# Linear attention numerators taken for two batches in one product with 128 weight columns

## Chip, cores and metric

One core of a Trainium2 chip runs the whole program. The metric is device time of that core in microseconds (us), the median over executions. Traces are of one profiled execution.

## What is computed

The input x is 8 batches of 512 rows of 128. Four layers follow one another, each added to x: a delta-rule attention, a mixture of 8 experts (top 2), a linear attention, and the same experts again. The change is in the third of them. Its reference, with 16 heads of 8 (`q`, `k` after elu + 1), over chunks of the rows:

```python
def step(carry, inp):
    S, z = carry
    q, k, v = inp
    A = jnp.einsum('bhid,bhjd->bhij', q, k) * mask
    num = jnp.einsum('bhij,bhjd->bhid', A, v) + jnp.einsum('bhid,bhde->bhie', q, S)
    den = jnp.sum(A, axis=-1) + jnp.einsum('bhid,bhd->bhi', q, z) + EPS
    out = num / den[..., None]
    S = S + jnp.einsum('bhjd,bhje->bhde', k, v)
    z = z + jnp.sum(k, axis=2)
    return ((S, z), out)
```

## The kernel before

The kernel works in 8 chunks (`NCH`) of 64 rows (`CH`) of all 8 batches, so a chunk is 512 tokens, held as 4 groups (`J`) of 128 partitions: two batches of 64 rows each. Its first half (up to about 566 us) runs the delta-rule attention with the first experts. Its second half, `step2(i)` for i = 0 to 8, runs the linear attention of chunk i (i = 0 to 7) interleaved by hand with the second experts of the chunk before. Every engine has its own instruction list, written in a fixed order, and the lists meet only in semaphores.

In TensorE's list of `step2`, `moe_up` (L1004 to L1006, three products with 512 moving columns for each half of the hidden layer) and `moe_down` (L1024, 8 products with 128 moving columns) of the 8 experts alternate with the parts of the linear attention. For each group j of two batches:

- `lin_scores` (L1138) makes the scores A of both batches, in four quarter-size tiles of the array, into two PSUM banks. Partition 64·par + s holds key row s of a head of parity par.
- VectorE's `lin_att` (L1598) multiplies them by the causal mask into `att` in SBUF.
- `lin_numer` (L1161, L1164) makes numerators and denominators. For each batch p of the two it takes 8 products (one for a pair of heads), with 64 weight columns (the rows of that batch) and 18 moving columns (two heads of 8 values and a one), and then one product of `phi_q` with the running state, with 64 weight columns and 144 moving columns. Batch p writes partitions 64·p to 64·p + 63 of a bank. All float32 products appear as two records in the trace, each with its own weight load.
- VectorE's `lin_out` (L1605, L1607, L1609) adds epsilon to the denominators, inverts them, and multiplies the numerators into `lin`.

The order on TensorE around these is: scores(0) after the q-side masks of VectorE (L1591); experts; scores(1), numer(0); experts; scores(2), numer(1), scores(3); experts; numer(2), numer(3); `moe_up(5)`; `lin_state` (L1173, the update of the state), `lin_transpose` (L1180); experts; and at the end of the step `moe_transpose` (L986), `lin_project` of the next chunk (L1102, L1106), `moe_route` (L992). VectorE's order is att(0), att(1), out(0), att(2), out(1), att(3), statistics of the next chunk, out(2), out(3), `lin_state` (L1616, L1620). TensorE's `lin_numer(3)` waits for out(1), `lin_state` for out(2), `lin_transpose` for out(3).

Of the kernel before, what the change touches and what calls it, by code (L numbers as in the profile page):

```python
# [27 lines left out]
ALU = mybir.AluOpType  # L28
# [4 lines left out]
H, HD = 16, 8  # L33
# [3 lines left out]
CH = 64  # L37
NCH = L // CH
NT = B * CH
J = NT // 128  # L40
# [5 lines left out]
HV = HD + 1  # L46
NP = H // 2
LN_EPS, DELTA_EPS, LIN_EPS = 1e-5, 1e-6, 1e-5
# [3 lines left out]
def due(count):  # L52

    return not isinstance(count, int) or count > 0


def held(eng, count):

    return count if isinstance(count, int) else eng.snap(eng.to_reg(count))


def bc(ap, axis, n):

    ap = ap.unsqueeze(axis)
    shape = list(ap.shape)
    shape[axis] = n
    return ap.to_broadcast(shape)


def build(nc, d, out):  # L70
    with ExitStack() as ctx:
        def sb(name, shape, dtype=F32):
            return ctx.enter_context(nc.sbuf_tensor(name, shape, dtype))

        def sem(name):
            return ctx.enter_context(nc.semaphore(name))
# [55 lines left out]
        prod_mem = sb("prod_mem", [128, CH * HD * HV])  # L132
# [52 lines left out]
        phi_q = hist_mem[:, HD * NT:(HD + 1) * NT]  # L185
        v_bd = sb("v_bd", [128, B, NP, 2, HV])
        att_size, ktok_size, state_size = 2 * NP * 2 * CH, B * D, B * H * HV
        att = prod_mem[:, 0:att_size].rearrange("p (k r b i t) -> p k r b i t", k=2, r=2, b=2, i=4)
        k_tok = prod_mem[:, att_size:att_size + ktok_size].rearrange("p (b f) -> p b f", b=B)
        dstate = prod_mem[:, att_size + ktok_size:att_size + ktok_size + state_size].rearrange(  # L190
            "p (b h e) -> p b h e", b=B, h=H)
        state = sb("state", [128, B, H, HV])
        den = sb("den", [128, J, H])
        rden = sb("rden", [128, J, H])
        lin_at = [slice(oq_size + NT * k, oq_size + NT * (k + 1)) for k in range(3)]
        lin = oq_mem[:, lin_at[0]].rearrange("p (j d) -> p j d", j=J)
# [3 lines left out]
        bank = ctx.enter_context(nc.psum_tensor("bank", [128, 8, 512], F32))  # L200
        TB, QB, KB, MB, XB, ZB, YB = 0, 1, 2, 3, 4, 5, 7
# [56 lines left out]
        att_ready, numer, den_ready = sem("att_ready"), sem("numer"), sem("den_ready")  # L258
        rden_ready, lin_ready = sem("rden_ready"), sem("lin_ready")
# [662 lines left out]
        def _(pe):  # L922
# [200 lines left out]
            def lin_scores(c, j):  # L1123

                if j == 0:
                    taken = held(pe, c + 1)
                    pe.wait_ge(go, 1)
                    pe.wait_ge(qbd_ready, taken)
                else:
                    read = held(pe, J * c + j)  # L1130
                    pe.wait_ge(go, 1)
                    pe.wait_ge(att_ready, read)
                for p in range(2):
                    b = 2 * j + p
                    for par in range(2):
                        for r in range(2):
                            h = slice(64 * r, 64 * r + 64)
                            last = nc.tensor.matmul(  # L1138
                                bank[64 * par:64 * par + 64, QB + r, 256 * p:256 * p + 256],
                                phi_k[h, b, 0], q_bd[h, par::2, CH * b:CH * b + CH],  # L1140
                                start=True, stop=True)
                last.then_inc(scores, 1)

            def lin_numer(c, j):

                pe.wait_ge(att_ready, J * c + j + 1)
                if j == 0:
                    pe.wait_ge(v_ready, 2 * (c + 1))
                    pe.wait_ge(ktok_ready, 2 * (c + 1))
                    if due(c):  # L1150
                        pe.wait_ge(state_ready, c)
                if j >= 2:
                    if due(J * c + j - 1):
                        pe.wait_ge(lin_ready, J * c + j - 1)
                for p in range(2):
                    b = 2 * j + p
                    o = bank[64 * p:64 * p + 64, (TB, MB)[j % 2], 0:H * HV]
                    for r in range(2):
                        for i4 in range(4):
                            n = 4 * r + i4  # L1160
                            nc.tensor.matmul(o[:, 2 * HV * n:2 * HV * n + 2 * HV], att[:, j % 2, r, p, i4],  # L1161
                                             v_bd[:, b, n].rearrange("p r e -> p (r e)"), start=(n == 0), stop=False,
                                             skip_group_check=True)
                    last = nc.tensor.matmul(o, phi_q[:, CH * b:CH * b + CH], state[:, b].rearrange("p h e -> p (h e)"),  # L1164
                                            start=False, stop=True, skip_group_check=True)
                last.then_inc(numer, 1)

            def lin_state(c):

# [25 lines left out]
            def step2(i, lin=True, pre=True):  # L1195
# [6 lines left out]
                if lin:  # L1202
                    lin_scores(i, 0)
                moe_expert(n, 2)
                if lin:
                    lin_scores(i, 1)
                    lin_numer(i, 0)
                moe_expert(n, 3)
                if lin:
                    lin_scores(i, 2)  # L1210
                    lin_numer(i, 1)
                    lin_scores(i, 3)
                moe_expert(n, 4)
                if lin:
                    lin_numer(i, 2)
                    lin_numer(i, 3)
# [22 lines left out]
            o, n = NCH - 1, NCH - 2  # L1239
# [21 lines left out]
        def _(dve):  # L1261
            tt, ts, stt, red = (nc.vector.tensor_tensor, nc.vector.tensor_scalar, nc.vector.scalar_tensor_tensor,
                                nc.vector.tensor_reduce)
# [330 lines left out]
            def lin_att(c, j):  # L1594
                dve.wait_ge(scores, J * c + j + 1)
                if due(J * c + j - 1):
                    dve.wait_ge(numer, J * c + j - 1)
                tt(att[:, j % 2].rearrange("p r b i t -> p (r b i) t"),  # L1598
                   bank[:, QB:QB + 2, :].rearrange("p r (n t) -> p (r n) t", t=CH),
                   bc(causal[:], 1, 16), ALU.mult).then_inc(att_ready, 1)  # L1600

            def lin_out(c, j):
                dve.wait_ge(numer, J * c + j + 1)
                src = bank[:, (TB, MB)[j % 2], 0:H * HV].rearrange("p (h e) -> p h e", h=H)
                ts(den[:, j], src[:, :, HD], LIN_EPS, None, ALU.add).then_inc(den_ready, 1)  # L1605
                dve.wait_ge(den_ready, J * c + j + 1)
                nc.vector.reciprocal(rden[:, j], den[:, j]).then_inc(rden_ready, 1)  # L1607
                dve.wait_ge(rden_ready, J * c + j + 1)
                tt(lin[:, j].rearrange("p (h e) -> p h e", h=H), src[:, :, 0:HD], bc(rden[:, j], 2, HD), ALU.mult  # L1609
                   ).then_inc(lin_ready, 1)  # L1610

            def lin_state(c):
                dve.wait_ge(state_parts, c + 1)
# [23 lines left out]
            def step2(i, lin=True, pre=True, src=x3):  # L1637
# [3 lines left out]
                if lin:  # L1641
                    lin_att(i, 0)
                moe_add(n, 0, src)
                if lin:
                    lin_att(i, 1)
                    lin_out(i, 0)
                if lin:
                    lin_att(i, 2)
                    lin_out(i, 1)
                    lin_att(i, 3)  # L1650
# [3 lines left out]
                if lin:  # L1654
                    lin_out(i, 2)
                    lin_out(i, 3)
# [25 lines left out]
            o, n = NCH - 1, NCH - 2  # L1682
# [75 lines left out]
```

## Time and profile before

| | |
|---|---|
| median of 3 runs | 993.63 us (992.57 to 994.19) |
| the profiled execution | 1000.56 us, of it a span of 998.8 us from first to last instruction |
| granted TensorE clock, mean over the span | 0.901 of full |
| TensorE products busy | 773.8 us, 77% |
| TensorE weight loads busy | 638.8 us, 64% |
| VectorE busy | 693.7 us, 69% |
| ScalarE busy | 547.9 us, 55% |
| GpSimd busy | 397.5 us, 40% |

Busy times are sums over instructions of one engine. Products on TensorE are pipelined: a record's duration is longer than the distance from its start to the next one's start, and it is this distance that the engine's list costs. Records in different tiles of the array overlap.

### The profile page before, as it was taken

Reading aid. Unit: us, or ns where it says so; the run is one execution under the profiler, and the core shown is the slowest. Engines: PE = TensorE matmul, PEld = TensorE weight load, DVE = VectorE, ACT = ScalarE, POOL = GpSimd, SP = SyncE. Lnnn points to the kernel's source line nnn. Section 1 sums busy time; section 2 is a strip of 40 time slices with the busy share of each in tenths; the row PEclk is TensorE's granted clock in tenths of the full one; section 3 lists DMA queues with packets and bytes.
Section 4 is the critical chain, followed back from the end, with each engine's and each line's share of the span. In section 5 each row is a group of like instructions: output and inputs, shape, how many; then the busy total and the mean of one; then the engine's idle time right before and its main releaser. Section 6 shows DMA issues by size and latency. Waiting matters only on the chain.

```text
span 998.8 us, 17238 instructions
## 1 busy us (share of the span) xinstructions
PE 773.8 (77%) x5736; PEld 638.8 (64%) x5736; DVE 693.7 (69%) x1420; ACT 547.9 (55%) x1505; POOL 397.5 (40%) x409
## 2 busy tenths in 40 slices
PE   2645145866768678576677899999999999999997
PEld 1423034755647556465565788787878787878786
DVE  1149999979889797999985547474747474747450
ACT  5574347577585866643455736363636363636355
POOL 1075887676856768576564101010101010101012
PEclk9767587988899879987879999999999999999999
DMA  4221211104021030210201000000000000000000
GB/s 134 73 76 34 55 53 47 63 0 120 1 69 49 0 108 0 71 39 0 64 1 43 1 23 1 23 1 21 0 21 0 21 0 21 0 21 0 12 5 18
DMA packets 48589, 32.17 MB, mean 32 GB/s; under 512 B 37664, under 2 KB 38944, under 8 KB 48288
## 3 DMA queue, kind: packets, MB, share of 16 engines
q1 hardware_dynamic: 48544, 31.61, 10.9%
q8 instruction: 23, 0.38, 0.2%
q14 instruction: 22, 0.18, 0.0%
HBM read 18.76 MB, written 12.85 MB: 32 GB/s over the span
## 4 chain that ended last, share of the span: by engine, by line
PE 41%; DVE 31%; ACT 12%; issue 10%; POOL 2%; DMA 2%; SPq 0%; DVEq 0%; ACTq 0%; POOLq 0%
PE bank L1024 14%; PE bank L1161 5%; DVE prod_mem L1320 4%; DVE hist_mem L1591 3%; PE bank L1004 3%; DVE u L1325 3%; PE bank L1138 3%; DVE hist_mem L1333 3%; DVE x L1460 3%; PE bank L1005 3%; PE bank L1006 3%; DVE hist_mem L1329 3%; ACT y_even L718 2%; PE bank L939 2%; PE bank L1173 2%
## 5 line engine op out<-in xcount | busy, mean ns | idle before, releaser
L1024 PE MATMUL bank<-w,hid 128*128 128x128 f32 x2048 | 275.0, 292 | 92.3 <-ACT y_even L718 81.4
L1024 PEld LDWEIGHTS bank<-w,hid 128*128 128x128 f32 x2048 | 263.8, 206 | 112.1 <-issue 62.3
L521 POOL TENSOR_TENSOR x_odd<-x_odd,y_odd 128x512 f32<-128x512 f32 x48 | 61.4, 1280 | 455.6 <-ACT y_odd L718 455.6
L695 ACT ACTIVATE hid<-bank 128x512 f32<-128x512 f32 x256 | 143.3, 601 | 95.7 <-PE bank L1006 92.9
L509 POOL TENSOR_TENSOR oq_mem<-hist_mem,q_p 128x384 f32<-128x384 f32 (+1 forms) x96 | 138.1, 1478 | 0.0
L1004 PE MATMUL bank<-xT_h,w_h 128*128 128x512 f32 x256 | 117.5, 459 | 3.7 <-ACT hid L695 3.2
L718 ACT ACTIVATE y_even<-bank,gate_now 128x128 f32<-128x128 f32 x256 | 73.2, 371 | 70.6 <-DVE gate_now L1450 34.5
L1005 PE MATMUL bank<-xT_l,w_h 128*128 128x512 f32 x256 | 103.2, 403 | 0.0
L1006 PE MATMUL bank<-xT_h,w_l 128*128 128x512 f32 x256 | 102.8, 402 | 0.0
L1460 DVE TENSOR_TENSOR x<-y_even,x 128x512 f32<-128x512 f32 x48 | 56.1, 1168 | 40.3 <-ACT y_even L718 40.2
L1320 DVE TENSOR_TENSOR prod_mem<-hist_mem,bank 128x256 f32<-128x256 f32 x128 | 78.2, 611 | 3.4
L1598 DVE TENSOR_TENSOR prod_mem<-bank,causal 128x1024 f32<-128x1024 f32 x32 | 39.2, 1225 | 54.5 <-PE bank L1138 53.4
L1004 PEld LDWEIGHTS bank<-xT_h,w_h 128*128 128x128 f32 x256 | 50.6, 197 | 30.6 <-issue 12.2
L939 PE MATMUL bank<-xnT_h,wtap_h 128*128 128x512 f32 x104 | 48.6, 468 | 25.7 <-issue 16.7
L1333 DVE TENSOR_REDUCE hist_mem<-hist_mem 128x64 f32<-128x320 f32 x128 | 62.1, 485 | 3.5
L1161 PEld LDWEIGHTS bank<-v_bd,prod_mem 128*64 128x64 f32 x1024 | 57.9, 138 | 7.1 <-issue 6.2
L1161 PE MATMUL bank<-v_bd,prod_mem 128*64 128x18 f32 x1024 | 60.3, 212 | 0.0
L1325 DVE TENSOR_REDUCE u<-prod_mem 128x32 f32<-128x288 f32 x128 | 57.3, 448 | 2.2
L718 ACT ACTIVATE y_odd<-bank,gate_now 128x128 f32<-128x128 f32 x192 | 54.9, 376 | 4.6 <-PE bank L1024 4.5
L1006 PEld LDWEIGHTS bank<-xT_h,w_l 128*128 128x128 f32 x256 | 49.7, 194 | 11.8
L1329 DVE TENSOR_TENSOR hist_mem<-u,bank 128x256 f32<-128x256 f32 x128 | 53.7, 420 | 3.7
L1005 PEld LDWEIGHTS bank<-xT_l,w_h 128*128 128x128 f32 x256 | 50.5, 197 | 7.4 <-issue 1.4
(162 smaller groups left out, 1432.1 us busy)
## 6 DMA issues: line engine op xcount, KB each, us to landing
s_qkv<-qkv SPq DMA_DIRECT2D x24, 256.0 KB, 3.4
pin<-s_qkv SPq DMA_DIRECT2D x16, 256.0 KB, 2.7
x_in<-in_x SPq DMA_DIRECT2D x8, 256.0 KB, 2.8
q_p<-s_qkv SPq DMA_DIRECT2D x8, 256.0 KB, 3.2
s_o<-o_p SPq DMA_DIRECT2D x8, 256.0 KB, 2.0
o_T<-s_o SPq DMA_DIRECT2D x8, 256.0 KB, 2.8
x_r<-in_x SPq DMA_DIRECT2D x8, 256.0 KB, 2.9
s_x<-x_odd SPq DMA_DIRECT2D x8, 256.0 KB, 2.4
```

The lines of the kernel that those rows point to most:

```text
L509: tt(oq[:, :, j, :, 0:HD], s_at, bc(q_step[:, :, j, n].rearrange("p d n -> p n d"), 2, HD), ALU.mult).then_inc(o_part, 1)
L695: nc.scalar.activation(hid[:, e % 2, f], bank[:, ZB + f, :], ACT.Relu).then_inc(hid_ready, 1)
L718: last = nc.scalar.activation((x_odd if e == 1 else y_odd if e % 2 else y_even)[:, j], bank[:, y_bank(e, wide), 128 * j:128 * j + 128], AC ...
L1004: nc.tensor.matmul(bank[:, ZB + f, :], w1_h[:, e, part], xT_h[:], start=True, stop=False)
L1005: nc.tensor.matmul(bank[:, ZB + f, :], w1_h[:, e, part], xT_l[:], start=False, stop=False)
L1006: nc.tensor.matmul(bank[:, ZB + f, :], w1_l[:, e, part], xT_h[:], start=False, stop=True).then_inc(z_ready, 1)
L1024: last = nc.tensor.matmul(bank[:, y_bank(e, wide), tokens], hid[:, e % 2, f, tokens], w2[:, e, f], start=(f == 0), stop=(f == FC - 1))
L1161: nc.tensor.matmul(o[:, 2 * HV * n:2 * HV * n + 2 * HV], att[:, j % 2, r, p, i4], v_bd[:, b, n].rearrange("p r e -> p (r e)"), start=(n == ...
L1320: tt(prod[:, t, :, 0:HD].rearrange("p t m d -> p m d t"), bc(hist[:, n, :, :, BS], 3, BS), bc(nw[:, :, t], 1, HD), ALU.mult).then_inc(step, 1)
L1325: red(u[:, n].rearrange("p m s -> p s m"), prod[:, BS * n:BS * n + BS], AX_X, ALU.add).then_inc(step, 1)
L1333: red(hist[:, n + 1, :, :, BS], hist[:, n], AX_X, ALU.add).then_inc(step, 1)
L1460: tt(x2[:], y_even[:], src if src is x3 else src[:], ALU.add).then_inc(added, 1)
```

## The change

In `att` the order of the axes becomes head pair, batch, row, so that the rows of both batches lie side by side for each head pair. `lin_numer` takes one product for a head pair with 128 weight columns (rows of both batches) and 36 moving columns (values of both batches); the quarter in which rows of one batch meet values of the other is computed and not read. The state product takes both batches too, with 128 weight columns and 288 moving columns in runs of 18. `lin_scores` writes to the new places with the same products. `lin_out` reads each half of the partitions apart, so two instructions stand for one twice.

```diff
-        att = prod_mem[:, 0:att_size].rearrange("p (k r b i t) -> p k r b i t", k=2, r=2, b=2, i=4)
+        att = prod_mem[:, 0:att_size].rearrange("p (k r i b t) -> p k r i b t", k=2, r=2, b=2, i=4)
...
-                                bank[64 * par:64 * par + 64, QB + r, 256 * p:256 * p + 256],
+                                bank[64 * par:64 * par + 64, QB + r].rearrange("p (i b t) -> p i b t", i=4, b=2)[:, :, p],
...
-                for p in range(2):
-                    b = 2 * j + p
-                    o = bank[64 * p:64 * p + 64, (TB, MB)[j % 2], 0:H * HV]
-                    for r in range(2):
-                        for i4 in range(4):
-                            n = 4 * r + i4
-                            nc.tensor.matmul(o[:, 2 * HV * n:2 * HV * n + 2 * HV], att[:, j % 2, r, p, i4],
-                                             v_bd[:, b, n].rearrange("p r e -> p (r e)"), start=(n == 0), stop=False,
-                                             skip_group_check=True)
-                    last = nc.tensor.matmul(o, phi_q[:, CH * b:CH * b + CH], state[:, b].rearrange("p h e -> p (h e)"),
-                                            start=False, stop=True, skip_group_check=True)
-                last.then_inc(numer, 1)
+                o = bank[:, (TB, MB)[j % 2], 0:2 * H * HV]
+                both = slice(2 * j, 2 * j + 2)
+                for n in range(NP):
+                    nc.tensor.matmul(o[:, 4 * HV * n:4 * HV * n + 4 * HV], att[:, j % 2, n // 4, n % 4].rearrange("p b t -> p (b t)"),
+                                     v_bd[:, both, n].rearrange("p b r e -> p b (r e)"), start=(n == 0), stop=False,
+                                     skip_group_check=True)
+                nc.tensor.matmul(o, phi_q[:, 2 * CH * j:2 * CH * j + 2 * CH],
+                                 state[:, both].rearrange("p b (n r) e -> p n b (r e)", r=2),
+                                 start=False, stop=True, skip_group_check=True).then_inc(numer, 1)
...
-                tt(att[:, j % 2].rearrange("p r b i t -> p (r b i) t"),
+                tt(att[:, j % 2].rearrange("p r i b t -> p (r i b) t"),
...
-                src = bank[:, (TB, MB)[j % 2], 0:H * HV].rearrange("p (h e) -> p h e", h=H)
-                ts(den[:, j], src[:, :, HD], LIN_EPS, None, ALU.add).then_inc(den_ready, 1)
-                dve.wait_ge(den_ready, J * c + j + 1)
+                src = bank[:, (TB, MB)[j % 2], 0:2 * H * HV].rearrange("p (n b r e) -> p n b r e", n=NP, b=2, r=2)
+                for p in range(2):
+                    own = slice(64 * p, 64 * p + 64)
+                    ts(den[own, j].rearrange("p (n r) -> p n r", r=2), src[own, :, p, :, HD], LIN_EPS, None, ALU.add
+                       ).then_inc(den_ready, 1)
+                dve.wait_ge(den_ready, 2 * (J * c + j + 1))
                 nc.vector.reciprocal(rden[:, j], den[:, j]).then_inc(rden_ready, 1)
                 dve.wait_ge(rden_ready, J * c + j + 1)
-                tt(lin[:, j].rearrange("p (h e) -> p h e", h=H), src[:, :, 0:HD], bc(rden[:, j], 2, HD), ALU.mult
-                   ).then_inc(lin_ready, 1)
+                for p in range(2):
+                    own = slice(64 * p, 64 * p + 64)
+                    last = tt(lin[own, j].rearrange("p (n r e) -> p n r e", n=NP, r=2), src[own, :, p, :, 0:HD],
+                              bc(rden[own, j].rearrange("p (n r) -> p n r", r=2), 3, HD), ALU.mult)
+                last.then_inc(lin_ready, 1)
```

## Rows read from the trace of the kernel before

**Rows 1.** The page: the span.
```profile
span 998.8 us, 17238 instructions
```

**Rows 2.** Stretch by stretch: length, busy us (records) of each engine, clock, DMA.
```profile
680.00:740.00 60.00, 58.04 (x610) 48.86 (x606) 34.55 (x83) 27.45 (x72) 5.09 (x4) 1.00 0.03 9
```

**Rows 3.** Waits of TensorE from 566 us on: in total, times, longest.
```profile
PE bank L1138 <- DVE hist_mem L1591: 8.3, 7, 1.2
PE bank L1119 <- ACT v_bd L798: 5.9, 8, 0.8
```

**Rows 4.** A group of TensorE by shape, from 560 us on: busy us, mean ns.
```profile
L1161 PE MATMUL bank<-v_bd,prod_mem 128*64 128x18 f32 x1024 | 60.3, 212 | 0.0
```

**Rows 5.** Timeline of TensorE, one linear attention step: start us, length us, records.
```profile
680.82 1.13 PE L1161 MATMUL bank<-v_bd,prod_mem 128*64 128x18 f32 x18
681.77 0.32 PE L1164 MATMUL bank<-state,hist_mem 128*64 128x144 f32 x1
...
683.32 0.39 PE L1005 MATMUL bank<-xT_l,w_h 128*128 128x512 f32 x1
...
687.38 1.13 PE L1161 MATMUL bank<-v_bd,prod_mem 128*64 128x18 f32 x18
...
689.54 1.09 PE L1138 MATMUL bank<-hist_mem,phi_k 64*64 64x256 f32 x16
...
692.07 1.95 PE L1024 MATMUL bank<-w,hid 128*128 128x128 f32 x16
693.94 1.13 PE L1161 MATMUL bank<-v_bd,prod_mem 128*64 128x18 f32 x18
...
698.13 0.39 PE L1005 MATMUL bank<-xT_l,w_h 128*128 128x512 f32 x1
...
699.29 2.12 PE L1173 MATMUL bank<-v_bd,prod_mem 128*128 128x144 f32 x16
701.25 0.60 PE L1180 MATMUL bank<-ident,oq_mem 128*128 128x128 f32 x4
...
713.41 1.15 PE L1106 MATMUL bank<-wv_b,oq_mem 128*64 128x64 f32 x32
714.50 1.06 PE L992 MATMUL bank<-wg,xfT 128*128 128x8 f32 x8
715.41 2.03 PE L1024 MATMUL bank<-w,hid 128*128 128x128 f32 x16
```

**Rows 6.** The chain that ended last: start us, us, what.
```profile
611.92 1.72 PE bank L1102 x4
...
683.05 0.43 PE bank L1004
...
701.84 1.79 PE bank L1024 x16
703.63 0.23 PE bank L1004
...
963.25 2.63 PE bank L1024 x16
```

**Rows 7.** Timeline of VectorE, same step, with the idle time before and its releaser.
```profile
683.09 0.17 DVE L1605 TENSOR_SCALAR den<-bank 128x16 f32<-128x16 f32 x1 [0.91 <-PE bank L1164]
...
683.59 0.29 DVE L1609 TENSOR_TENSOR oq_mem<-bank,rden 128x128 f32<-128x128 f32 x1
...
690.71 1.23 DVE L1598 TENSOR_TENSOR prod_mem<-bank,causal 128x1024 f32<-128x1024 f32 x1 [0.27 <-PE bank L1138]
...
698.40 0.29 DVE L1609 TENSOR_TENSOR oq_mem<-bank,rden 128x128 f32<-128x128 f32 x1
701.45 1.49 DVE L1616 TENSOR_TENSOR prod_mem<-bank,state_mask 128x432 f32<-128x432 f32 x3 [2.76 <-PE bank L1173]
```

**Rows 8.** Stretch view of the end of the span, columns as in rows 2.
```profile
950.00:999.00 49.00, 41.08 (x285) 37.45 (x283) 15.00 (x37) 25.93 (x74) 8.89 (x7) 0.92 0.03 12
```

## The prediction

> **What bounds the kernel.** I first read the page for the span, 998.8 us [rows 1]. The change touches only the linear attention, which lies behind 566 us, so I read the stretches there: of 60 us TensorE has products in 58.04, VectorE is busy in 34.55 and ScalarE in 27.45, at a granted clock of 1.00, the 2.4 GHz level [rows 2]. Then the waits: in the whole second half TensorE waits 8.3 us for the masks of L1591 and 5.9 us for `v_bd` [rows 3]. Both waits are at the head of a step; between scores(0) and the last transpose TensorE waits for nobody, and the chain that ended last runs through its list there. So whatever `lin_numer` gains or loses in TensorE's list goes to the end at full size, 8 times (steps 0 to 7).
>
> The busy sums mislead. L1161 has 60.3 us at 212 ns a record [rows 4], but durations overlap. What counts is start to start [rows 5]. Numer(0) goes from 680.82 to about 682.98, numer(1) from 687.38 to 689.54, numer(2) and (3) from 693.94 to about 697.79: some 8.2 us in a step, 65 us in all.
>
> **What a record costs.** In one batch 16 records of L1161 go from 680.82 to 681.77: 0.059 us each, with 64 weight columns and 18 moving ones [rows 5]. What sets this? Three rows with 128 weight columns tell. L992, with 8 moving columns: 714.50 to 715.41 for 8 records, 0.114 us (the first is the slow one after another tile size). L1024, with 128 moving columns: 1.79 us for 16 in the chain, 0.112 each [rows 6]. L1173, with 144: 699.29 to 701.25 for 16, 0.1225. So 8 and 128 moving columns cost alike, 0.112, and only above that does the price grow with the moving columns. For few moving columns the price is that of the weight columns: 0.059 for 64, 0.112 for 128, hardly less than double.
>
> **The change on TensorE, for each group j.** It removes 32 records of 0.059 and 4 state records. It adds 16 records with 128 weight columns and 36 moving ones. 36 lies between L992's 8 and L1024's 128, which agree, so I take 0.112, 16 x 0.112 = 1.79. It adds two state records with 288 moving columns. Price: L1173 gives 0.1225/144 = 0.85 ns a column, L1102 (512 columns) 1.72/4 = 0.43 us, 0.84 ns a column [rows 6]; so 0.243 each, 0.49 for both. Sum 2.28 against the some 2.04 of before (8.17/4): the halves of the array before hid part of the state product behind the other batch, which the wide form can't.
>
> **Changes of tile size.** These move too. L1024 to L1161 (128 columns to 64): 692.07 to 693.94 is 1.87 for 16 records [rows 5], where the same 16 take 1.79 before a full-size follower [rows 6]: about 0.09 of draining. After such a change the first load isn't hidden either. The chain shows both together on L1004: 0.43 behind numer(0), 0.23 behind L1024 [rows 6]. For the first wide record after the scores I take 0.02 of it (L992's mean of 0.114 against 0.112, over 8 records). The wide form has the size of the experts' products, so:
>
> - numer(0), measured from its first record to L1005. Before: 680.82 to 683.32 = 2.50. After: 16 x 0.112 + 0.02 (first load unhidden) + 2 x 0.243 + L1004 0.23 = 2.53. +0.03. The drain in front (after the scores) stays.
> - numer(1), first record to the next scores. Before: 687.38 to 689.54 = 2.16. After: 1.81 + 0.243 + 0.243 + 0.10 of draining = 2.40. +0.23.
> - numer(2) and (3), from L1024's first record to L1005. Before: 692.07 to 698.13 = 6.06. After: 1.79 + 2 x (1.79 + 0.486) + 0.23 = 6.57; no change of size is left here. +0.51.
>
> Sum +0.77 us in a step, x 8 = **+6.2 us**. Without the two changes of size that it saves (0.2 each, after numer(0) and numer(3)) it would be some +1.2 in a step.
>
> One row bears on what the wide form gives up. L1106 has 64 weight columns as L1161 has, but alternates between the two halves of the array record by record: 713.41 to 714.50 for 32, 0.034 each, against 0.059 for L1161, which stays in one half for a whole batch [rows 5]. The Trainium skill has the rule ("TensorEngine Tiling (Array Packing)", Key Properties): tiles are independent, and different ones load weights and multiply at the same time. The trace agrees for L1106, and for numer only at the seam between two batches, since the list goes batch by batch. Read without the trace, the rule would put the narrow numer(j) at half, some 1.1 us, and the loss at 1.2 x 4 x 8 = 38 us; the kernel before doesn't take that gain, so the sum stays at 6.2.
>
> **Edits at nothing.** Scores: same products, same 64-column runs, other places in the bank; L1138 is bound by 256 moving columns. `lin_att`: same 1024 contiguous elements. The layout of `att` costs the load nothing, since L1024 and L992 load 128 contiguous columns too.
>
> `lin_out` gets two more instructions: at most another 0.17 and 0.29 us (its durations for all 128 partitions, taken again for half of them) [rows 7], 0.46 x 32 = 14.7 us of VectorE. At overlapped pace rather 0.3 each, 10 us. I cost it at nothing, because of who waits: out(3) ends at 698.69 and `lin_transpose` wants it at 701.25, 2.6 us later [rows 5, 7], while VectorE then sits 2.76 us waiting for L1173 [rows 7]. Out(2) ends still earlier, and L1173, which waits for it, starts at 699.29. Out(1) stands before att(3), which today waits only 0.27 us for its scores [rows 7]; it would start up to 0.2 us later, and end near 692.2, but numer(3) wants it half way from 693.94 to 697.8. Behind att(3) the statistics delay ScalarE's `rstd`, and so the expert activation behind it, by as much; TensorE wants that only in `moe_up(5)`, near 697.8. If all this cover were gone, it would cost the 10 to 14.7 us.
>
> The 288 moving columns come in runs of 18 where before 144 were contiguous. No row has runs of 18 that bind. L1138's moving side has 4 runs of 64 and shows no loss. Bounds: nothing, or at most the state product doubled, 0.486 x 4 x 8 = 15.6 us. I take nothing, by L1138.
>
> **Sum.** In the profiled execution the span goes from 998.8 to 1005.0 and its time from 1000.56 to 1006.8. It lies 6.9 us above the median of 993.63, which has nothing to do with this stage; so the median goes to 993.63 + 6.2 = **999.8 us**.
>
> **Rivals.**
>
> *Faster: a record costs its floor, whatever its weights' width.* If the pace of 0.059 is a price per record and not of 64 columns, 64 records a step at 0.059 instead of 0.112 save 3.4 us against my sum: 0.77 - 3.4 = -2.6 a step, -21 us, 972.6 us. It decides from a price under 0.100 us for a wide record (0.112 - 0.77/64). Against it: L992 at 0.112 with 8 moving columns. For it: only that no row has 36. Chance 5%. The Trainium skill has a rule of this kind ("TensorEngine Tiling (Array Packing)", Instruction Overhead): some 60 cycles for any matmul of up to 60 free columns; it would be 25 ns here, and neither L1161 nor L992 shows it.
>
> *No change within 0.2%*: the loss shrinks to under 2 us, because the wide list lets something start earlier, say scores(3), or the wait for L1591 shrinks. Against it: these waits hang on the end of TensorE's list and move with it. Chance 6%.
>
> *Slower by more: runs of 18 read slowly*, up to +15.6 us on top, 1015. A record of L1164 would then start up to 0.49 us before the next instead of 0.243. Chance 6%.
>
> *Slower by more: VectorE comes to bind* through att(3) or out(3), 10 us on top, 1010. Against it the cover above. Chance 5%.
>
> A smaller unsure thing is the clock at the end: 0.92 over the last 49 us [rows 8], since it falls to the 1.2 GHz level in part of them, behind TensorE's wait for the last routing (16 records of L1024 take 2.63 us there instead of 1.79 [rows 6]); all of this shifts by 6 us, and may cost or give back 1 us.
>
> **How the numbers follow.** The forecast case has 78%: 993.63 + 6.2, with 1 us either way for the clock, 1 for the start of records after a change of size, and 1 for run to run (the three runs span 1.6). It reaches from 996.5 to 1003. The range leaves out the fast rival and the far ends of the slow ones: 996.0 to 1004.0. 0.2% is 2.0 us, about what a measurement of this kernel can tell from no change: faster 6%, same 8%, slower 86%, some of each for what I don't see.
>
> **What would show it.** L1161 as 512 records 0.112 us apart, 36 moving columns. L1164 as 64 records, 0.243 us apart (twice that would be the rival). The distances of numer(0), numer(1), numer(2) with (3) as above: 2.53, 2.40, 6.57. The step longer by 0.8 us. L1004 after numer at 0.23 in the chain instead of 0.43. VectorE with 64 more instructions and the wait before L1616 shorter by no more than 1 us. The prediction is wrong if wide records start under 0.100 us apart, or if TensorE gets a wait between scores(0) and the last transpose.

## The result and the profile after

| | before | changed |
|---|---|---|
| median, first timing | 993.1 us (991.85 to 994.19, 4 runs) | 1004.65 us (1002.98 to 1009.51, 4 runs) |
| ratio | | 1.0106, 95% interval 1.0063 to 1.0149 |
| median, timed again | 996.78 us (993.82 to 1003.09, 18 runs) | 1005.24 us (1003.08 to 1011.41, 7 runs) |
| ratio | | 1.0079, 95% interval 1.0048 to 1.0111 |
| profiled execution, span | 998.8 us | 1001.2 us |

The change makes the kernel slower, by 0.6 to 1.5% in the first timing and 0.5 to 1.1% in the second, with more runs. I had forecast +6.2 us (0.6%). The spans differ by only 2.4 us, and that is a trap; see below.

The chain that ended last in the changed kernel, at the masks that end each step (start us, us, what):

```profile
666.97 4.93 DVE hist_mem L1588 x7
...
717.85 4.92 DVE hist_mem L1588 x7
...
768.72 4.92 DVE hist_mem L1588 x7
```

A step takes 50.87 us. The kernel before has the same piece here:

```profile
670.34 4.92 DVE hist_mem L1591 x7
...
919.95 4.92 DVE hist_mem L1591 x7
```

That is 5 steps, 49.92 us each. So +0.95 us a step, 7.6 us in 8 steps.

The timeline of TensorE in one step of the changed kernel, beside [rows 5]. L1158 is the numerator product (L1161 before), L1161 the state product (L1164 before), L1170 and L1177 the old L1173 and L1180:

```profile
674.54 1.95 PE L1024 MATMUL bank<-w,hid 128*128 128x128 f32 x16
676.42 1.09 PE L1138 MATMUL bank<-hist_mem,phi_k 64*64 64x256 f32 x16
677.45 1.97 PE L1158 MATMUL bank<-v_bd,prod_mem 128*128 128x36 f32 x16
679.25 0.73 PE L1161 MATMUL bank<-state,hist_mem 128*128 128x288 f32 x2
679.61 0.61 PE L1004 MATMUL bank<-xT_h,w_h 128*128 128x512 f32 x1
680.06 0.40 PE L1005 MATMUL bank<-xT_l,w_h 128*128 128x512 f32 x1
...
684.13 1.98 PE L1158 MATMUL bank<-v_bd,prod_mem 128*128 128x36 f32 x16
685.94 0.73 PE L1161 MATMUL bank<-state,hist_mem 128*128 128x288 f32 x2
686.60 1.09 PE L1138 MATMUL bank<-hist_mem,phi_k 64*64 64x256 f32 x16
...
689.13 1.95 PE L1024 MATMUL bank<-w,hid 128*128 128x128 f32 x16
690.91 1.87 PE L1158 MATMUL bank<-v_bd,prod_mem 128*128 128x36 f32 x16
692.61 0.73 PE L1161 MATMUL bank<-state,hist_mem 128*128 128x288 f32 x2
693.19 1.87 PE L1158 MATMUL bank<-v_bd,prod_mem 128*128 128x36 f32 x16
694.89 0.73 PE L1161 MATMUL bank<-state,hist_mem 128*128 128x288 f32 x2
695.24 0.61 PE L1004 MATMUL bank<-xT_h,w_h 128*128 128x512 f32 x1
695.69 0.40 PE L1005 MATMUL bank<-xT_l,w_h 128*128 128x512 f32 x1
```

| distance | before | forecast | measured | change forecast | change measured |
|---|---|---|---|---|---|
| numer(0), first record to L1005 | 2.50 | 2.53 | 680.06 - 677.45 = 2.61 | +0.03 | +0.11 |
| numer(1), first record to scores | 2.16 | 2.40 | 686.60 - 684.13 = 2.47 | +0.23 | +0.31 |
| numer(2), (3), L1024 to L1005 | 6.06 | 6.57 | 695.69 - 689.13 = 6.56 | +0.51 | +0.50 |

Together +0.92 of the step's +0.95. Half as many numerator records, each about twice as far apart: 677.45 to 679.25 for 16 is 0.1125. The waits of TensorE behind 566 us (in total, times, longest) are those of before [rows 3], so nothing new is waited for:

```profile
PE bank L1138 <- DVE hist_mem L1588: 8.4, 7, 1.2
PE bank L1119 <- ACT v_bd L798: 5.8, 8, 0.8
```

**The trap in the spans.** The first product of L1138, in step 0 of the linear attention, starts at 575.6 us in the profile of before and at 570.3 in that of the changed kernel. The first half of both programs is the same code, up to its place in memory. Over thirteen profiles of this study that start lies between 563.9 and 575.6 us. From it to the end the runs repeat closely: 423.2 us before and 423.2 with only the division split; 430.8 to 430.9 in three profiles with the wide products (the changed kernel twice, and once with the simpler division of the experiments). So the change is worth +7.7 us there, whatever a single span says. The medians of before, which were taken on several chips, wander by 3.7 us from one timing to another; the scatter of the first half may be the reason, but the runs without a profile can't be taken apart.

### The profile page after: what moved, and what is told of

Its sections match the earlier page's. It is cut to its first block, busy times and chain, and to the rows that moved or that the text cites. A ratio compares the mean times of both kernels' runs of the same rounds, so it can differ in the third digit from the quotient of the medians.

```text
span 1001.2 us, 16174 instructions
## 1 busy us (share of the span) xinstructions
PE 780.9 (78%) x5160; PEld 646.2 (65%) x5160; DVE 701.6 (70%) x1484; ACT 546.3 (55%) x1505; POOL 399.2 (40%) x409
## 4 chain that ended last, share of the span: by engine, by line
PE 43%; DVE 29%; ACT 13%; issue 10%; POOL 2%; DMA 1%; DVEq 0%; SPq 0%; ACTq 0%; POOLq 0%
PE bank L1024 15%; PE bank L1158 6%; DVE hist_mem L1588 3%; DVE prod_mem L1317 3%; PE bank L1138 3%; DVE u L1322 3%; PE bank L1004 3%; DVE hist_mem L1330 3%; PE bank L1005 3%; PE bank L1006 3%; DVE hist_mem L1326 3%; PE bank L939 2%; ACT y_even L718 2%; DVE x L1457 2%; PE bank L1161 2%
## 5 line engine op out<-in xcount | busy, mean ns | idle before, releaser
L1024 PE MATMUL bank<-w,hid 128*128 128x128 f32 x2048 | 274.5, 291 | 86.7 <-ACT y_even L718 76.7
L1024 PEld LDWEIGHTS bank<-w,hid 128*128 128x128 f32 x2048 | 263.0, 205 | 106.6 <-issue 58.6
L1004 PE MATMUL bank<-xT_h,w_h 128*128 128x512 f32 x256 | 118.7, 464 | 4.0 <-ACT hid L695 3.5
L1005 PE MATMUL bank<-xT_l,w_h 128*128 128x512 f32 x256 | 102.8, 402 | 0.0
L1457 DVE TENSOR_TENSOR x<-y_even,x 128x512 f32<-128x512 f32 x48 | 47.4, 988 | 40.2 <-ACT y_even L718 40.2
L1004 PEld LDWEIGHTS bank<-xT_h,w_h 128*128 128x128 f32 x256 | 50.5, 197 | 28.7 <-ACT hid L695 12.3
L1158 PEld LDWEIGHTS bank<-v_bd,prod_mem 128*128 128x128 f32 x512 | 60.2, 192 | 7.1 <-issue 6.2
L1158 PE MATMUL bank<-v_bd,prod_mem 128*128 128x36 f32 x512 | 61.5, 277 | 0.0
L1005 PEld LDWEIGHTS bank<-xT_l,w_h 128*128 128x128 f32 x256 | 50.1, 196 | 8.3 <-issue 1.4
```

The costliest lines, as they stand in the source:

```text
L1004: nc.tensor.matmul(bank[:, ZB + f, :], w1_h[:, e, part], xT_h[:], start=True, stop=False)
L1005: nc.tensor.matmul(bank[:, ZB + f, :], w1_h[:, e, part], xT_l[:], start=False, stop=False)
L1024: last = nc.tensor.matmul(bank[:, y_bank(e, wide), tokens], hid[:, e % 2, f, tokens], w2[:, e, f], start=(f == 0), stop=(f == FC - 1))
L1158: nc.tensor.matmul(o[:, 4 * HV * n:4 * HV * n + 4 * HV], att[:, j % 2, n // 4, n % 4].rearrange("p b t -> p (b t)"), v_bd[:, both, n].rear ...
```

## The experiments

Eleven runs, all compared with the kernel before on the same chip.

**The change timed again.** No edit.

> The changed kernel, timed again in more rounds beside the kernel before. My theory: all of the loss is in the four numerator groups of a step, whose distances in the first profile add up to +0.93 us a step, 8 steps, +7.5 us, ratio 1.0075. The median of the first timing, +11.5 us, has 4 us more; if these are real and belong to the change, the ratio stays near 1.0115 and the part before the second half (566 us) would have to be longer in the changed kernel; if they are scatter of the first half, the ratio falls towards 1.0075 and the profile's step stays at 50.87 us.

Measured: ratio 1.0079 (1.0048 to 1.0111), step 50.87 us, 430.8 us from the first L1138 to the end. The interval holds 1.0075 and leaves out the 1.0115 of the rival, and the profile has almost nothing beyond the steps. So the surplus of the first median doesn't belong to the change. That it was scatter of the first half is the likely reading; no profile of the long runs exists that would show it.

**VectorE's part alone, and the change without it.** The kernel before with the division split:

```diff
-                ts(den[:, j], src[:, :, HD], LIN_EPS, None, ALU.add).then_inc(den_ready, 1)
+                for p in range(2):
+                    own = slice(64 * p, 64 * p + 64)
+                    ts(den[own, j], src[own, :, HD], LIN_EPS, None, ALU.add).then_inc(den_ready, 1)
...
+                for p in range(2):
+                    own = slice(64 * p, 64 * p + 64)
+                    last = tt(lin[own, j].rearrange("p (h e) -> p h e", h=H), src[own, :, 0:HD], bc(rden[own, j], 2, HD), ALU.mult)
```

> The kernel before with nothing but the division taken apart by halves of the partitions (64 more VectorE instructions). Theory (covered by TensorE's list): ratio 1.000, the wait before L1616 shorter by about 0.3 us, nothing else moves. Rival (VectorE's part of the change is on the path): up to +10 us, 1.010.

Measured: ratio 0.9989 (0.996 to 1.0018), step 49.92 us. The wait before L1616 shrank from 2.76 to 2.26 us, by 0.50 and not by the 0.3 that I had.

The changed kernel with one read for both halves:

```diff
-                for p in range(2):
-                    own = slice(64 * p, 64 * p + 64)
-                    ts(den[own, j].rearrange("p (n r) -> p n r", r=2), src[own, :, p, :, HD], LIN_EPS, None, ALU.add
-                       ).then_inc(den_ready, 1)
+                ts(den[:, j].rearrange("p (n r) -> p n r", r=2), src[:, :, 0, :, HD], LIN_EPS, None, ALU.add).then_inc(den_ready, 1)
...
+                tt(lin[:, j].rearrange("p (n r e) -> p n r e", n=NP, r=2), src[:, :, 0, :, 0:HD],
+                   bc(rden[:, j].rearrange("p (n r) -> p n r", r=2), 3, HD), ALU.mult).then_inc(lin_ready, 1)
```

> The changed kernel, but the division is two single instructions over all 128 partitions, which read the numerators of the first batch of each group for both halves (the second batch's numerators are left out). Theory: the same step of 50.87 us as the changed kernel, ratio to before near 1.0075. Rival (VectorE's part costs): back by up to 10 us, ratio near 1.000.

Measured: ratio 1.0085 (1.0054 to 1.0115), step 50.87 us (masks at 667.42 and 718.29). VectorE's part is free both ways. It is not small, though. The timeline of VectorE in the changed kernel (idle before it and its releaser in brackets):

```profile
686.71 0.38 DVE L1604 TENSOR_SCALAR den<-bank 64x16 f32<-64x16 f32 x2 [1.22 <-PE bank L1161]
687.12 0.25 DVE L1607 RECIPROCAL rden<-den 128x16 f32<-128x16 f32 x1
687.40 0.59 DVE L1611 TENSOR_TENSOR oq_mem<-bank,rden 64x128 f32<-64x128 f32 x2
688.02 1.23 DVE L1595 TENSOR_TENSOR prod_mem<-bank,causal 128x1024 f32<-128x1024 f32 x1
...
699.01 1.49 DVE L1619 TENSOR_TENSOR prod_mem<-bank,state_mask 128x432 f32<-128x432 f32 x3 [2.07 <-PE bank L1170]
```

An instruction over 64 partitions takes about what one over 128 takes, and the second doesn't overlap the first: 0.38 instead of 0.17, 0.59 instead of 0.29 [rows 7], +0.51 us for each division, more than the 0.46 that I had called the most. Att(3) at 688.02 no longer waits for its scores but for the division. The cover holds all the same: numer(3) starts at 693.19.

**The narrow products in alternation.** The kernel before with the two batches inside the loop over head pairs, and their two state products side by side behind it:

```diff
-                for p in range(2):
-                    b = 2 * j + p
-                    o = bank[64 * p:64 * p + 64, (TB, MB)[j % 2], 0:H * HV]
-                    for r in range(2):
-                        for i4 in range(4):
+                halves = [(2 * j + p, bank[64 * p:64 * p + 64, (TB, MB)[j % 2], 0:H * HV]) for p in range(2)]
+                for n in range(NP):
+                    for p, (b, o) in enumerate(halves):
                             nc.tensor.matmul(o[:, 2 * HV * n:2 * HV * n + 2 * HV], ...)
-                    last = nc.tensor.matmul(o, phi_q[:, CH * b:CH * b + CH], ...)
+                for b, o in halves:
+                    last = nc.tensor.matmul(o, phi_q[:, CH * b:CH * b + CH], ...)
```

> The kernel before, with 64 weight columns, but the products of the two batches alternate record pair by record pair, as those of L1106 do. Theory (two halves of the array load weights and multiply at the same time, the list before gave them no chance): a pair of records, one in each half, every 0.058 us, so 16 pairs take 0.93 us instead of 1.9; with the state products side by side numer(0) to L1005 takes about 1.7 us instead of 2.50, numer(1) 1.3 instead of 2.16, numer(2) and (3) 2.4 instead of 3.85: -3.1 us a step, -25 us, ratio 0.975. Rival (the weight path takes one load at a time and 18 moving columns are too few to hide one): 0.059 us a record as before, ratio 1.000.

Measured: ratio 0.9729 (0.9695 to 0.9763), median 969.94 us. TensorE's timeline (L1158 and L1162 are the two kinds of product here):

```profile
663.53 1.11 PE L1158 MATMUL bank<-v_bd,prod_mem 128*64 128x18 f32 x32
664.48 0.45 PE L1162 MATMUL bank<-state,hist_mem 128*64 128x144 f32 x4
664.86 0.50 PE L1004 MATMUL bank<-xT_h,w_h 128*128 128x512 f32 x1
665.19 0.39 PE L1005 MATMUL bank<-xT_l,w_h 128*128 128x512 f32 x1
...
669.24 1.11 PE L1158 MATMUL bank<-v_bd,prod_mem 128*64 128x18 f32 x32
670.20 0.45 PE L1162 MATMUL bank<-state,hist_mem 128*64 128x144 f32 x4
670.75 1.09 PE L1138 MATMUL bank<-hist_mem,phi_k 64*64 64x256 f32 x16
```

The same 32 records go from 663.53 to 664.48: 0.030 us each instead of 0.059. Numer(0) to L1005 is 1.66 us instead of 2.50. The rival (one weight load at a time) falls, and with it any reading in which 0.059 is a floor for a record. Numer(1) gains 0.65, not 0.85: scores(3) has caught up with the mask of group 2, which VectorE ends at 670.61 and behind which L1138 starts at 670.75. The step is 47.08 us (masks at 700.14 and 747.22), -2.84.

**What paces a wide record.** First the state product's moving side in plain order (the numerators of the state part come out misplaced):

```diff
-                                 state[:, both].rearrange("p b (n r) e -> p n b (r e)", r=2),
+                                 state[:, both].rearrange("p b h e -> p (b h e)"),
```

> The changed kernel, but the moving side of the state product is read as 288 contiguous columns instead of runs of 18 (heads of the two batches then add into the wrong numerators). In the changed kernel the first state record comes 0.330 us before the second, and the second 0.243 us before the next product. Theory (the 0.087 us is the first record's own weight load, which a stream of records bound by loads can't hide, since it stands 0.112 us behind a product of only 36 columns): unchanged, 0.330 and 0.243, step 50.87 us. Rival (runs of 18 read slower): 0.243 and 0.243, step shorter by 0.35 us.

One run, 1002.25 us. In its trace:

```profile
678.85 0.73 PE L1161 MATMUL bank<-state,hist_mem 128*128 128x288 f32 x2
679.65 0.39 PE L1005 MATMUL bank<-xT_l,w_h 128*128 128x512 f32 x1
```

0.80 us from the first state record to L1005, against 0.81 in the changed kernel. Read by single records the first state record stands 0.325 us before the second, where the changed kernel has 0.330. The step is 50.82 us, shorter by 0.05 and not by the rival's 0.35. Runs of 18 cost at most some 0.005 us a record; that rival falls.

Then 18 moving columns in place of 36 (the second batch's values are left out):

```diff
-                    nc.tensor.matmul(o[:, 4 * HV * n:4 * HV * n + 4 * HV], ...
-                                     v_bd[:, both, n].rearrange("p b r e -> p b (r e)"), ...
+                    nc.tensor.matmul(o[:, 4 * HV * n:4 * HV * n + 2 * HV], ...
+                                     v_bd[:, 2 * j, n].rearrange("p r e -> p (r e)"), ...
```

> The changed kernel, but each product takes only the 18 moving columns of the first batch (values of the second batch are left out). Theory (a wide record is paced by its 128 weight columns): still 0.112 us from record to record, step 50.87 us within 0.1; the first state record even 0.345 us before the second, since a product of 18 columns covers less of its load. Rival (the moving columns set part of the pace): 0.008 us a record less (18 columns at 0.84 ns and a half of it), step shorter by 0.5 to 1 us.

Measured: one run of 1012.4 us, where the changed kernel has medians of 1004.65 and 1005.24. The chain has the masks at uneven distances, and the stretches between them (length, busy us and records of PE, PEld, DVE, ACT, POOL, granted clock, DMA share, GB/s) say why:

```profile
617.50:671.60 54.10, 52.15 (x401) 44.38 (x400) 32.86 (x86) 23.87 (x63) 5.10 (x4) 0.94 0.03 11
671.60:724.00 52.40, 50.45 (x401) 42.83 (x400) 32.74 (x85) 23.82 (x63) 5.11 (x4) 0.97 0.03 10
724.00:774.90 50.90, 48.95 (x402) 41.64 (x401) 32.84 (x85) 23.92 (x64) 5.11 (x4) 1.00 0.03 10
774.90:825.80 50.90, 48.95 (x402) 41.63 (x400) 32.84 (x86) 23.91 (x63) 5.11 (x4) 1.00 0.03 10
```

Where the clock stays at the 2.4 GHz level (1.00), the step is the changed kernel's. So the moving columns don't set the pace: 18 or 36, 0.112 us. But in other steps the clock falls to the 1.2 GHz level; TensorE's timeline shows it in numer(3), behind three quarters of the step's numerator records and more than 20 us behind the step's last wait (scores(0), at 676.63):

```profile
696.76 0.60 PE L1158 MATMUL bank<-v_bd,prod_mem 128*128 128x18 f32 x4
697.21 0.73 PE L1161 MATMUL bank<-state,hist_mem 128*128 128x288 f32 x2
697.78 2.06 PE L1158 MATMUL bank<-v_bd,prod_mem 128*128 128x18 f32 x16
699.67 1.31 PE L1161 MATMUL bank<-state,hist_mem 128*128 128x288 f32 x2
700.37 1.04 PE L1004 MATMUL bank<-xT_h,w_h 128*128 128x512 f32 x1
```

The state pair takes 1.31 us instead of 0.73. My guess of 0.345 us between the state records was wrong too: it is 0.331, as with 36 columns.

The same kernel once more:

> The wide kernel with 18 moving columns in each numerator product, a second look (the second batch's numerators are left out). In the first look the granted clock fell in some steps (0.94 and 0.97 of full over these steps) and these took 52.4 to 54.1 us, the others 50.87 us. If that belongs to this kernel's thinner work, it falls again in some steps; if it was chance, all steps have 50.87 us at clock 1.00, as the changed kernel's have.

1012.77 us, and the same pattern: 54.10 us at clock 0.94, 52.5 at 0.97, 50.9 at 1.00. It was not chance: in each of the two profiles the clock falls in five of the eight steps. The last section has one more such fall, with 36 columns.

**Quarters.** Alternate, with 32 weight columns and four parts of the array in turn:

```diff
-                halves = [(2 * j + p, bank[64 * p:64 * p + 64, (TB, MB)[j % 2], 0:H * HV]) for p in range(2)]
+                quarters = [(2 * j + s // 2, s // 2, 32 * (s % 2), bank[32 * s:32 * s + 32, (TB, MB)[j % 2], 0:H * HV])
+                            for s in range(4)]
...
-                    for p, (b, o) in enumerate(halves):
+                    for b, p, t, o in quarters:
-                        nc.tensor.matmul(..., att[:, j % 2, n // 4, p, n % 4],
+                        nc.tensor.matmul(..., att[:, j % 2, n // 4, p, n % 4, t:t + 32],
...
-                    last = nc.tensor.matmul(o, phi_q[:, CH * b:CH * b + CH], ...
+                    last = nc.tensor.matmul(o, phi_q[:, CH * b + t:CH * b + t + 32], ...
```

> The alternating kernel one division further: 32 weight columns a product, four quarters of the array in turn (twice the records). Theory (each quarter loads and multiplies on its own, 32 columns take half of the 0.058 us that 64 take): four records every 0.03 us, 16 rounds of them in 0.47 us where alternate takes 0.95 us, about 0.45 us less for each group, but numer(1) gains nothing since scores(3) already waits for the mask of group 2; step about 1.35 us shorter than alternate's 47.08, 11 us in all, ratio to before 0.962. Rival (a floor for each record in the queue, of the 0.030 us that alternate already shows from record to record): 64 records in 1.9 us, all of alternate's gain gone, ratio 1.000.

Measured: ratio 0.9685 (0.9629 to 0.9741). Median 964.62 us. In the timeline:

```profile
675.04 0.71 PE L1159 MATMUL bank<-v_bd,prod_mem 128*32 128x18 f32 x62
675.58 0.29 PE L1163 MATMUL bank<-state,hist_mem 128*32 128x144 f32 x1
...
676.55 1.09 PE L1138 MATMUL bank<-hist_mem,phi_k 64*64 64x256 f32 x16 [0.51 <-DVE prod_mem L1597]
```

Twice the records in about half the time: 62 in 0.54 us, 0.009 each, four in 0.035. No floor of 0.030 for a record. The step is 45.92 us (masks at 659.24 and 705.16); I had 45.73, and TensorE's 0.51 us wait before scores(3) is now plain.

Timed once more beside alternate:

> Quarters timed again beside alternate. Step 45.92 against 47.08, so 9.3 us less than alternate and 32 us less than before: ratio 0.968.

> Alternate timed again beside quarters: 22.7 us less than before by the steps, ratio 0.977; the first timing said 0.973.

Measured: quarters 0.9661 (0.9624 to 0.9698), median 961.7 us; alternate 0.9752 (0.971 to 0.9794), median 970.86 us. Quarters is the faster by both.

**Quarters without the wait.**

```diff
-                    lin_scores(i, 3)
-                moe_expert(n, 4)
+                moe_up(n, 4)
+                if lin:
+                    lin_scores(i, 3)
+                moe_down(n, 3)
```

> Quarters, with scores(3) moved behind the first half of the next expert (moe_up(4)), so that it no longer waits 0.51 us for the mask of group 2. It buys that with two more changes of tile size, 0.2 to 0.3 us together beyond the drain that it saves. Theory: step 45.7 us against 45.92, 2 us in all, within the interval of quarters. Rival: a change of tile size costs less than the 0.2 us I read on L1004, then step 45.4.

Measured: ratio 0.966 (0.9619 to 0.9701), median 960.89 us; step 45.58 us (masks at 657.49 and 703.07). The wait is gone from TensorE's list, and two thirds of it are kept, 0.34 of 0.51 us, between my two figures. By time it can't be told from quarters.

## Why the prediction came out as it did

The direction, the cause and the place were right. The numerator groups are the whole change, TensorE's list passes them on in full in each of 8 steps, and a record with 128 weight columns starts 0.112 us after the last. The size was a fifth short: +0.77 us a step forecast, +0.95 measured, 6.2 against 7.6 us. The term that fell short is the state product's.

- **Price of the numerator records.** Forecast 0.112, measured 0.112. Right, and the run with 18 moving columns shows directly that 18 or 36 don't matter to it.
- **Price of the state records.** Here is the mis-sized term. I gave both 0.243 us. The second has it; the first takes 0.330. The surplus of 0.087 comes where the stream of short products ends in this long one, four times a step. The trace of before had the like: behind L992, with 8 columns, 16 records of L1024 take 1.79 us from the first start to that of L1004 (715.41 to 717.20), where behind L1180 they take 1.71 (701.68 to 703.39); the first two starts stand 0.192 us apart and not 0.112. In numer(2) and (3) it is given back at the entrance: from L1024 into the wide products 16 of them take 1.70 us (690.91 to 692.61), not 1.80 as behind the scores. That is why these two came out at 6.56 against 6.57, and numer(0) and (1) 0.08 and 0.07 too cheap. That the surplus is the product's own unhidden weight load was my explanation; it forecast 0.345 us with 18 columns, 0.331 was measured, and it falls. What the 0.087 is stays open.
- **Changes of tile size.** Saved where I said: L1004 costs 0.23 us in the chain behind numer(0) and numer(3), no longer 0.43. The drains stand as read, and quarters with scores(3) moved back bears out their order of size: two more changes of size there cost 0.17 us (0.51 less the 0.34 kept).
- **Scores, masks, layout, runs of 18 at nothing.** Right within 0.05 us a step; for the runs of 18 shown by the run with 288 contiguous columns. The other three were not tried by themselves; what the distances leave to all of them together is 0.03 us a step.
- **VectorE at nothing.** Right for the time, shown both ways, by the division split alone and by the changed kernel with one read. Its price was wrong: 16 us of busy time in all (0.51 x 32), where I had 10 and at most 14.7.
- **The clock at the end**, "may cost or give back 1 us". It changed nothing: from L992 behind the last routing to the end the changed kernel takes 36.7 us and the kernel before 36.6, and in both the clock falls in part of it.
- **What it shows by time.** The median moved by 11.5 us in the first timing, to 1004.65, just above the upper end of my range; +8.5 us in the second lies inside it. 7.6 us are in the steps. The rest I put down to scatter of the first half. I had allowed 1 us for run to run, and the first half alone differs by over 10 us from profile to profile. My range of 996 to 1004 was too narrow for that, and only the repeated timing and the distances inside the step separate the two.
- **The rival of no change** (a wait shrinks). The two waits at the head of the step are 8.4 and 5.8 us in all, where before had 8.3 and 5.9, and the second interval begins at 1.0048. It falls.
- **The fast rival** (a floor for each record whatever its width) is refuted three times: by the 0.112 of the wide form, the 0.030 of alternate, the 0.009 of quarters.
- **The rule on tiles** (the Trainium skill, "TensorEngine Tiling (Array Packing)", Key Properties: different tiles load and multiply at the same time). I had read it as a gain that the kernel before doesn't take, and put a price of 1.1 us on a numer(j) that would. Alternate has it at 0.95 for the numerator products and 1.33 with the state and the drain (663.53 to 664.86). The trace of alternate agrees with the rule, with 0.030 us a record for 0.059, and the rule spoke against this change: merging two narrow products into a wide one loads the same columns one after the other that two halves load at once.

## What to carry to other kernels

With few moving columns, and as long as the list stays in one part of the array, a float32 product costs what its weight columns cost (0.059 us for 64, 0.112 for 128). So merging two products of 64 weight columns into one of 128 saves nothing, however many records it saves; read the price from a row with as few moving columns and the width you want. If products go to different column parts of the array, write them in alternation: the same instructions in another order gave 2.5 to 2.7% here, and parts of 32 columns 3.4%, while the merged form lost 0.8%. Where an unchanged half of a program scatters by more than the effect, measure from a fixed instruction behind it to the end.

## What the runs showed that I had not expected

- The pace of records across column parts goes down to 0.009 us with 32 weight and 18 moving columns, 2048 records of it in the kernel, and TensorE's list keeps up.
- The granted clock can fall far from any wait of TensorE. With 128 weight columns and only 18 moving ones it fell to the 1.2 GHz level in five of eight steps (0.94 and 0.97 over a step, up to 3.2 us lost), in both profiles. In both profiles of the changed kernel, with 36, it stays at 1.00 through all eight steps. But 36 columns don't rule it out: in the run with 288 contiguous columns, otherwise the same work, the clock fell once, in the last step and at the same place, numer(3) (1.87 and 0.73 us elsewhere):

```profile
946.83 2.33 PE L1158 MATMUL bank<-v_bd,prod_mem 128*128 128x36 f32 x16
948.96 1.31 PE L1161 MATMUL bank<-state,hist_mem 128*128 128x288 f32 x2
```

  So the fall was seen in the wide form alone, in 10 of 16 steps with 18 columns and in one of the 32 of the four profiles with 36. What sets it off stays open. The narrow forms in alternation, with 18 columns and halves or quarters, keep 1.00 in all stretches read (quarters here):

```profile
700.00:780.00 80.00, 75.08 (x1131) 62.26 (x1132) 53.29 (x131) 40.51 (x103) 8.97 (x7) 1.00 0.04 13
```

- Alternate gains 24.2 us from the first L1138 to the end (423.2 to 399.0, in both profiles) where 8 steps of 2.84 us explain 22.7; quarters 33.6 where 8 steps of 4.0 explain 32.0. The remaining 1.5 us is the clock at the end. From the last L992 to the end of the span, first before and then alternate (columns as in rows 2):

```profile
962.20:998.80 36.60, 30.15 (x200) 27.28 (x200) 7.91 (x19) 19.06 (x54) 7.61 (x6) 0.90 0.04 15
927.86:962.90 35.04, 28.59 (x200) 25.97 (x200) 7.92 (x19) 18.99 (x54) 7.61 (x6) 0.98 0.04 16
```

  The same 200 records of TensorE take 1.56 us less. Before runs those behind the last routing in part at the 1.2 GHz level (16 records of L1024 take 2.63 us there), alternate at the 2.4 GHz level (1.89 us).
